# A conditional FFN on one core: first loads in another order, the last sequence's expert product inside its own wo, ranks turned two token tiles at a time

## The reference, cut to what matters

```python
# x: 8 sequences x 256 tokens x 256; F = 1024; rank 16; 8 experts; one expert id per sequence
h  = x @ wi.T
h += 2 * (x @ common_wi_a.T) @ common_wi_b.T
h += 2 * (x @ experts_wi_a[e].T) @ experts_wi_b[e].T      # e = expert of the sequence
h  = relu(h)
o  = h @ wo.T
o += 2 * (h @ common_wo_a.T) @ common_wo_b.T
o += 2 * (h @ experts_wo_a[e].T) @ experts_wo_b[e].T
return x + o
```

## Time and profile before

| | us |
|---|---|
| median of 3 runs (lowest, highest) | 123.06 (122.58, 123.3) |
| the profiled execution, its own time | 122.64 |
| its span, first to last instruction | 120.9 |
| PE busy | 113.3 |
| DVE, ACT, POOL busy | 53.5, 45.4, 41.2 |

### The profile page before, as it was taken

How to read it: one execution, slowest core, us unless ns; L and a number is a source line. 1 busy time by engine, 2 the same in 40 slices (tenths; PEclk the granted TensorE clock), 3 DMA queues, 4 the chain that set the end, 5 groups by cost and what they waited for, 6 DMA issues and landing times.

```text
span 120.9 us, 1964 instructions
## 1 busy us (share of the span) xinstructions
PE 113.3 (94%) x724; PEld 103.4 (86%) x724; DVE 53.5 (44%) x97; ACT 45.4 (38%) x93; POOL 41.2 (34%) x62
## 2 busy tenths in 40 slices
PE   6899949899999999999999999999999999999961
PEld 6688839678889999988889999988889999999950
DVE  4684899799954241134444331234444011111111
ACT  4552929944873411223663511313333111111120
POOL 2037761999999220215573005324000020200000
PEclk9999999999999999999999999999999999999999
DMA  2999899997480017106000025107000011111002
GB/s 85 384 242 350 285 384 346 386 304 249 98 319 0 5 46 217 35 11 217 0 5 0 0 57 163 43 5 216 1 0 0 0 46 46 43 43 42 22 22 87
DMA packets 8635, 14.52 MB, mean 120 GB/s; under 512 B 1026, under 2 KB 5122, under 8 KB 8626
## 3 DMA queue, kind: packets, MB, share of 16 engines
q1 hardware_dynamic: 7906, 13.09, 33.8%
q10 hardware_dynamic: 720, 1.31, 2.9%
HBM read 12.30 MB, written 2.10 MB: 119 GB/s over the span
## 4 chain that ended last, share of the span: by engine, by line
PE 76%; DVE 7%; ACT 6%; DMA 4%; SPq 4%; issue 1%; DVEq 0%
PE bank_o L654 40%; PE bank_h L567 23%; PE bank_h L601 5%; DMA b_raw<-in_rec_b 4%; DVE b_stack L458 3%; ACT hid L365 3%; ACT b_stack L353 2%; PE bank_o L673 2%; PE bank_low L618 2%; PE bank_o L567 1%; DVE low_stack L442 1%; PE bank_low L567 1%; DVE w_raw L480 1%; SPq L199 1%; PE bank_o L664 1%
## 5 line engine op out<-in xcount | busy, mean ns | idle before, releaser
L654 PE MATMUL bank_o<-wcat,hid 128*128 128x272 f32 x384 | 51.4, 290 | 0.0
L654 PEld LDWEIGHTS bank_o<-wcat,hid 128*128 128x128 f32 x384 | 49.7, 189 | 0.0
L567 PE MATMUL bank_h<-xT,wiT 128*128 128x512 f32 x156 | 39.7, 395 | 0.5 <-DVE wiT L512 0.5
L567 PEld LDWEIGHTS bank_h<-xT,wiT 128*128 128x128 f32 x156 | 28.1, 190 | 5.6 <-ACT xT L343 0.7
L442 DVE SCALAR_TENSOR_TENSOR hid<-bank_h,hid 128x512 fp32r<-128x512 f32 x26 | 17.3, 688 | 13.9 <-ACT hid L365 13.9
L502 DVE TENSOR_TENSOR o_sb<-bank_o,x_nat 128x256 f32<-128x256 f32 x16 | 6.8, 425 | 34.2 <-PE bank_o L673 34.2
L365 ACT ACTIVATE hid<-bank_h 128x512 fp32r<-128x512 f32 x26 | 14.8, 598 | 18.5 <-PE bank_h L601 18.2
L260 POOL TENSOR_TENSOR b_stack<-b_raw,b_stack 32x1024 fp32r<-32x1024 f32 x6 | 14.3, 2391 | 7.0 <-ACT b_stack L353 7.0
L278 POOL CAST wcat<-a_raw 128x128 fp32r<-128x128 f32 x8 | 2.3, 289 | 29.2 <-PE bank_o L654 29.1
L377 ACT ACTIVATE rank_sb<-bank_o 128x64 fp32r<-128x64 f32 x16 | 3.6, 225 | 22.3 <-PE bank_o L654 22.3
L601 PEld LDWEIGHTS bank_h<-low_stack,b_stack 128*128 128x128 f32 x52 | 8.7, 189 | 3.9 <-DVE low_stack L442 2.1
(11 more groups left out here) (50 smaller groups left out, 87.3 us busy)
## 6 DMA issues: line engine op xcount, KB each, us to landing
b_raw<-in_rec_b SPq DMA_DIRECT2D x8, 512.0 KB, 5.1
x_nat<-in_x_n SPq DMA_DIRECT2D x4, 512.0 KB, 5.3
out<-o_sb SPq DMA_DIRECT2D x16, 128.0 KB, 1.7
x_raw<-in_x_t SPq DMA_DIRECT2D x6, 256.0 KB, 3.2
w_raw<-in_wo_t SPq DMA_DIRECT2D x4, 256.0 KB, 6.1
w_raw<-in_wi_t ACTq DMA_DIRECT2D x3, 256.0 KB, 4.4
a_raw<-in_rec_a SPq DMA_DIRECT2D x8, 96.0 KB, 3.2
bo_raw<-in_rec_bo SPq DMA_DIRECT2D x8, 96.0 KB, 4.2
```

The costliest lines, as they stand in the source:

```text
L567: nc.tensor.matmul(up_bank(q, m)[:, :], wiT_at(sw, k, m), xT[q % 2][sx][:, k, :], start=start, stop=False)
L654: last = nc.tensor.matmul(bank_o[g % NO][:, 0:WIN], hid[q % 2][sh][:, m, tok], wcat[sw][:, m, win], start=(m == 0 and i == 0), stop=(m == ...
```

## The change

- **Loads.** SP issues the first half of wi before the expert ids. The three loads of `common` move from before `load_b(0)` to behind `load_a(1)`. On POOL `split_common` moves behind `split_a(1)`, and on DVE `common_b` moves from before the low parts of `b_stack` to behind the low parts of step 1's x.
- **Banks.** There are three `bank_h` and four `bank_o`; token tile t always uses `bank_o[t]`, and the up stages of steps 2 and 3 use `bank_o0` and `bank_o1` for tiles 3 and 4. `up_main(1, 1)` comes before `wo_product(0)`, and `wo_product(2)` and `(3)` behind `up_main(1, 2)`.
- **Turning by pairs.** `turn` runs once for two token tiles (ranks of both in one `rank_sb`), in the middle of the tile behind the pair, or for tiles 2 and 3 behind `ranks_in` or in the next step's first tile. Both `fin` of the pair follow. To pick a tile's ranks, `bo` is laid out as 512 columns with zeros (records of 96x512 in place of 96x256).
- **The last sequence.** `rec_ao` of the last sequence's expert is loaded into `common_raw`. In down 2 and down 3 eight matmuls `own_wo_product` make experts_wo_a x experts_wo_b, DVE adds it to what `w_raw` holds (wo with the common product), ACT and DVE split it into the no longer needed `wiT`. The last two token tiles then multiply with that wo: 256 columns, no ranks, no turn, no fin.
- `add` writes into `x_nat` in place, `o_sb` is gone, and `load_x_nat(q)` waits for the stores of step q - 2.

```diff
+            def load_last_ao():
+                sp.wait_ge(common_a_lo, 1)
+                sp.dma_start(common_raw[:, 0:F], rec_ao[bass.ds(expert[B - 1], 1), :, :].rearrange("o p c -> (o p) c")
+                             ).then_inc(last_ao_in, 16)
...
-            sp.dma_start(idt[:, :], ids.rearrange("(o n) -> o n", o=1)).then_inc(ids_in, 16)
             for k in range(KD):
                 sp.dma_start(w_raw[:, 0, k * 2 * P:(k + 1) * 2 * P], wi_t[0][:, k * 2 * P:(k + 1) * 2 * P]).then_inc(wi0_in[k], 16)
+                if k == 0:
+                    sp.dma_start(idt[:, :], ids.rearrange("(o n) -> o n", o=1)).then_inc(ids_in, 16)
...
+            def own_wo_product(i):
+                if i == 0:
+                    pe.wait_ge(last_ao_lo, 1)
+                    pe.wait_ge(bo_ready, B)
+                    pe.wait_ge(hid_lo, STEPS * MF)
+                for jj in range(2):
+                    m = 2 * i + jj
+                    last = nc.tensor.matmul(own_bank(i)[:, jj * D:(jj + 1) * D], common_st[:, m * P:(m + 1) * P],
+                                            bo_stack[(STEPS - 1) % 2][:, PAIR - 1, 0:D], start=True, stop=True)
                 last.then_inc(prod_done, 1)
...
             def down(q, before):
                 down_main(q, 0, FIRST_HALF)
                 if before is not None:
-                    turn(before, TT - 1)
+                    turn(before, 3)
+                    own_wo_product(3)
                 down_main(q, 0, SECOND_HALF)
                 if before is not None:
-                    fin(before, TT - 1)
-                for t in range(1, TT):
-                    down_main(q, t, FIRST_HALF)
-                    turn(q, t - 1)
-                    down_main(q, t, SECOND_HALF)
-                    fin(q, t - 1)
+                    fin(before, 2)
+                    fin(before, 3)
+                if q == 2:
+                    own_wo_product(0)
+                    own_wo_product(1)
+                down_main(q, 1)
+                down_main(q, 2, FIRST_HALF)
+                turn(q, 1)
+                if q == 2:
+                    own_wo_product(2)
+                down_main(q, 2, SECOND_HALF)
+                fin(q, 0)
+                fin(q, 1)
+                down_main(q, 3)
                 if q + 2 < STEPS:
                     ranks_in(q + 2, 0)
                     ranks_in(q + 2, 1)
-                    turn(q, TT - 1)
+                    turn(q, 3)
                     up_main(q + 2, 0)
-                elif q == STEPS - 1:
-                    turn(q, TT - 1)
-                    fin(q, TT - 1)
```

More of the change, by code:

```diff
@@ L15, with conditional_ffn @@
 STAGES = [("up", 0), ("up", 1), ("down", 0), ("up", 2), ("down", 1), ("up", 3), ("down", 2), ("down", 3)]
-def conditional_ffn(nc, x_t, x_n, ids, wi_t, wo_t, rec_a, rec_b, rec_bo, common, out):
+def conditional_ffn(nc, x_t, x_n, ids, wi_t, wo_t, rec_a, rec_b, rec_bo, rec_ao, common, out):
     P = 128
@@ L74, in up_bank_free @@
         def up_bank_free(q, m):
-            if q == 0:
+            if q == 0 or (q > 1 and m in (3, 4)):
                 return 0
@@ L196, in _ @@
                 load_a(0, n)
-            sp.wait_ge(common_zero, 1)
-            for i in range(3):
-                sp.dma_start(common_raw[i * BLK:i * BLK + R, :], common).then_inc(common_in, 16)
             load_b(0)
@@ L204, in _ @@
                 load_a(1, b)
+            sp.wait_ge(common_zero, 1)
+            for i in range(3):
+                sp.dma_start(common_raw[i * BLK:i * BLK + R, :], common).then_inc(common_in, 16)
             load_b(1)
@@ L518, in first_up @@
                     split_wi_lo(i)
-                common_b()
                 split_b_lo(0, 0)
@@ L524, in first_up @@
                     split_x_lo(1, k)
+                common_b()
                 for m in range(MF):
@@ L641, in down_main @@
                 if 0 in tiles:
-                    if t % SEQ_TILES == 0:
+                    if t % SEQ_TILES == 0 and not own_wo(g):
                         pe.wait_ge(ao_ready[b], q + 1)
-                    if g == 0:
-                        pe.wait_ge(hid_lo, MF + 4)
-                    if g >= NO:
+                    if q < STEPS - 1 and t < 2:
+                        pe.wait_ge(hid_lo, (q + 1) * MF + [3, 4][t] + (q > 0))
+                    elif g >= NO:
                         pe.wait_ge(added, g - NO + 1)
@@ L652, in down_main @@
                             pe.wait_ge(wo_lo, m // 2 + 1)
+                    if own_wo(g):
+                        if t % SEQ_TILES == 0 and m % 2 == 0:
+                            pe.wait_ge(wo_lo, PIECES + m // 2 + 1)
+                        for i, (sh, sw) in enumerate(((HI, HI), (HI, LO), (LO, HI))):
+                            last = nc.tensor.matmul(bank_o[t][:, 0:D], hid[q % 2][sh][:, m, tok], own_cols(sw, m // 2)[:, m % 2, :],
+                                                    start=(m == 0 and i == 0), stop=(m == MF - 1 and i == 2))
+                        continue
                     for i, (sh, sw) in enumerate(((HI, HI), (HI, LO), (LO, HI))):
-                        last = nc.tensor.matmul(bank_o[g % NO][:, 0:WIN], hid[q % 2][sh][:, m, tok], wcat[sw][:, m, win],
+                        last = nc.tensor.matmul(bank_o[t][:, 0:WIN], hid[q % 2][sh][:, m, tok], wcat[sw][:, m, win],
                                                 start=(m == 0 and i == 0), stop=(m == MF - 1 and i == 2))
@@ L711, in up @@
                     if m == 1:
+                        fin(before, TT - 2)
                         fin(before, TT - 1)
```

150 lines of the change are left out of this document (97 added, 53 removed).

## The result

The changed kernel is slower. Its median is 123.85 us (7 runs, 123.58 to 124.61) against 123.12 us for the kernel before on the same chip (7 runs), a ratio of 1.0087 with the interval [1.0047, 1.0127]. The forecast was 121.0 us, with 122.3 as the upper end of its range. Medians are over all runs, while the ratios leave out runs of a slower state (over 1.5% above the fastest of their kernel), so the two can differ. The execution that was profiled took 124.61 us and was the slowest of the seven; its span is 122.7 us, 1.8 us more than before.

What follows compares the result with a forecast made beforehand. PE, 94% busy at the full clock, was taken to set the time wherever it does not wait. Start -1.6, body -0.1, new wait +1.7 and tail -1.8 sum to -1.8: 122.85 - 1.8 = 121.0 us, range 119.4 to 122.3.

Steps and rivals of the forecast that it cites:

- The start: Up to up_lora(1, 0): earlier loads and the products 2 and 3 moved behind up matmuls give 1.6 us less.
- the third rival: At the start, common lands late and holds POOL up longer; slower than before, say 123.9 us; chance 0.04.
- One sign of being wrong: In the start: the forecast is wrong if hid_lo holds PE before 24 us.
- PE's body: PE's main work: eight turns fewer and narrower matmuls against eight own products, sum -0.1 us.
- The new wait: At ranks_in of step 3, PE waits 1.7 us for a_stack, whose reload stands behind step 1's first store.
- The tail: After the last main matmul: no turn, rank copies or fins of the last tile, 1.8 us less.
- The fourth: Rival: a wait in the own wo chain of down 2 or 3, about 1 us, 122.0; chance 0.09.
- The first, no new wait: Rival: a_stack of step 3 is in time after all, sum -3.5, about 119.3 us; chance 0.12.
- The second: Rival: the start gives only 0.4 to 0.9, common late or common_b caught by POOL, 121.8 to 122.4; chance 0.2.

Runs made afterwards that it cites:

- changed_again: The changed kernel without an edit, run again beside others of its group: 124.22 us, ratio 1.0076 to the kernel before.
- ids_first: The changed kernel with only the expert ids issued before the two halves of wi again: 123.42 us, ratio 0.9977.
- reload_ranks: reload_early plus, on DVE in the down stages, the ranks of tile 1 ahead of the second low part of x: 120.91 us, ratio 0.9801.
- ids_reload_ranks: reload_ranks with the expert ids issued first again: 119.68 us, ratio 0.9714.
- before_new_start: The kernel before with only the new order of loads, split_common and common_b: 123.28 us, ratio 1.0026.
- fill_no_own: fill without the last sequence's own wo; its last two token tiles go through ranks, turn and fin: 119.38 us, ratio 0.9717.
- fill_common_b: fill with DVE's common_b moved into the loop of the first hidden tiles, three tiles later: 120.66 us.
- fill: ids_reload_ranks with up_main(1, 2) ahead of up_lora(1, 0), up_lora(1, 1) right behind it, products 2 and 3 one tile later: 118.32 us, ratio 0.9593.
- ranks_first: The changed kernel with only DVE's ranks of tile 1 moved ahead of the second low part of x: 122.76 us, ratio 0.9984.
- reload_early: The changed kernel with step 3's a_raw reload issued ahead of the first store of step 1: 122.06 us, ratio 0.9952.
- start_as_before: ids_first with common also loaded, split and copied where the kernel before does it: 124.01 us, ratio 1.0055.

## Why the prediction was wrong, step by step

**The start** (forecast 1.6 us less, measured 0.7 more in the first trace and 0.2 less in the second) is the step that failed. It had `up_lora(1, 0)` at 24.5; it came at 26.74 and 25.87. Three things were wrong in it.

The first is its first sentence. I priced "the ids come about 0.4 us later (one DMA issue)". The issue did come 0.45 us later, but 32 bytes behind a load of 128 KB then took 2.37 us (the chain's row at 1.20), and 2.75 in changed_again. SP's reads of the ids, first before, then in the changed kernel:

```profile
L195 SPq TENSOR_LOAD <-idt x2: 274/373/472, 2.1 to 3.4; - x2
```

```profile
L213 SPq TENSOR_LOAD <-idt x2: 279/376/472, 3.6 to 4.9; - x2
```

So everything picked by the ids came 1.5 us late, which ate the whole 1.54 us that the moved `common` loads gave: `b_raw` issued at 6.17, not at 5.0. The issue of the last `common` began at 13.25; the 12.45 of the forecast is the end of that issue, so its start is 12.0, and it came 1.2 us late. Two pairs of kernels differ in the place of the ids alone (the changed kernel and ids_first, reload_ranks and ids_reload_ranks). By the ratios the ids cost 1.35 and 1.1 us there, at the gates of the traces 0.6 and 0.7. This is the largest part of the miss.

The second is an entry of POOL's list that no term has. The sum goes from the landing of `common` straight to POOL's 1.08 us, but `split_a(1)` stands in front, and waits for `a_raw` of step 1. In the changed kernel's trace:

```profile
17.52 0.32 POOL L273 TENSOR_TENSOR a_stack<-a_raw,a_stack 128x64 fp32r<-128x64 f32 x1
...
18.15 1.09 POOL L304 CAST common_st<-common_raw 96x1024 fp32r<-96x1024 f32 x1 [0.32 <-DMA common_raw<-in_common]
```

`split_a(1)` ends at 17.84, 1.9 us past the 15.9 at which the forecast has POOL begin with `common`, and POOL then waits only 0.3 us more. In changed_again, ids_first and before_new_start it does not wait for `common` at all. What this entry costs depends on when `a_raw` lands: in five traces with the ids first, POOL begins with `common` at 16.77 (ids_first), 16.59 (ids_reload_ranks), 16.20 (fill_no_own), 15.43 (fill_common_b) and 15.23 (fill), on both sides of the forecast 15.9. No run moves `split_a(1)` alone, so this part is read from traces and not from a comparison.

The third is the landing. The rows count it from the start of an issue, and the forecast added it to the end: from the start, "I take 15.9" leaves 3.9 us for the last `common`. It took 4.8 in the first trace, as long as the longest of the kernel before. It landed at 18.03, past the 17.7 that the third rival gave as the point where nothing is left, and that rival had a chance of 0.04. But its mechanism is the smallest part: POOL was not free before 17.84, so the landing cost 0.3 us in this trace and nothing in the second.

What came before the gate went as forecast. DVE's two low parts took 1.22 us each (forecast 1.35). In changed_again `up_lora(0, 0)` starts at 15.54 without a wait (forecast 15.4); in the first trace it starts at 17.81 because of slow matmuls (last section). One sign of being wrong that I had named did show: in changed_again `hid_lo` holds PE for 0.55 us at `ranks_in(1)`, at 19.54, because `common_b` ended at 18.67 and not before 17.5. The wait at the gate behind it hides that.

**The turns** are the step that was not there. Of the own wo I wrote that "I followed down 2 and down 3"; down 0 and down 1 I did not follow. There DVE has both low parts of step q + 2's x between the ranks of tile 0 and those of tile 1, and the second waits for ACT's `xT` copy, which stands behind ACT's own ranks of tile 1. While each tile had a turn of its own, a late `rank_sb` had half a tile to hide in; with pairs, the turn wants tile 1's ranks half a tile behind it. The timeline of the changed kernel shows the order:

```profile
44.47 0.77 DVE L487 TENSOR_TENSOR xT<-x_raw,xT 128x512 fp32r<-128x512 f32 x1 [2.04 <-ACT xT L360]
45.16 0.16 DVE L482 SCALAR_TENSOR_TENSOR rank_sb<-bank_o,rank_sb 128x16 fp32r<-128x16 f32 x1
```

The two downs take 0.48 and 0.34 us more than in fill, 0.8 together (0.9 in changed_again); ranks_first took them away and gained 0.87 in the trace.

**PE's body** was right: forecast -0.1. In fill, where PE does not wait from down 0 on, down 0 is 0.33 shorter than before, down 1 0.34, down 2 and 3 0.22 longer, up 2 and up 3 0.12 longer each for their second fin: -0.2 us.

**The new wait** was right in kind, place and cause, and within reach in size: forecast 1.7 (1.5 to 1.9), measured 2.11, and 1.56 in the second trace. The links are all there, from the add that lets the store go to the reload behind it and `a_stack` at last:

```profile
74.48 0.75 DVE L557 TENSOR_TENSOR x_nat<-bank_o,x_nat 128x256 f32<-128x256 f32 x2 [2.07 <-PE bank_o L768]
74.94 0.33 SPq L204 DMA_DIRECT2D out<-x_nat  x1
...
75.52 0.89 SPq L180 DMA_DIRECT2D a_raw<-in_rec_a  x2
...
78.85 0.34 POOL L270 CAST a_stack<-a_raw 128x192 fp32r<-128x192 f32 x1 [0.56 <-DMA a_raw<-in_rec_a]
```

The second record's load landed late here, with 0.56 us of POOL waiting between the two; in changed_again POOL went from one to the next at once. Taking the wait away gave 1.8 us (reload_early).

**The tail** was right: forecast 1.8 less, measured 4.49 - 2.65 = 1.84. The own wo as a whole is worth 1.1 us by the medians of fill_no_own and 0.9 in its trace, since its products cost PE on the way.

**The other rivals.** The fourth, a wait in the own wo's chain, did not come up: no row of waits names `wiT` in down 2 or 3. The first, no new wait, fell with the trace. The second was not the case in the changed kernel: DVE's operation took 1.14 us there, as in the earlier trace rows, beside POOL's short operation of 1.09 and not the long one. It did come in one execution of fill, whose lists have the same order there.

The terms as measured: start +0.7, body -0.2, turns +0.8, the reload's wait +2.1, `ranks_in` behind it +0.2 (1.19 against 0.96), tail -1.8. That is +1.8, and it is the difference of the two spans. In the second trace: start -0.2, body -0.2, turns +0.9, wait +1.6, `ranks_in` +0.2, tail -1.8, together +0.5. Between them lie the two sets of runs, with +1.1 and +0.9 us by their ratios. Against the forecast of -1.8 the start is the largest miss in both traces (2.3 and 1.4 us), the turns the second.

## What to carry to other kernels

Ask of each load what waits for its value, not how large it is: a few bytes that choose the addresses of later loads belong first on their queue, and their price is a landing behind whatever is ahead, not an issue. When a landing is followed into an engine, count every entry that stands ahead in that engine's list, with its own waits: here it was POOL's `split_a(1)` and not the landing that set the gate. When two steps are merged into one, the merged step wants the later of its inputs at the earlier time, so follow it in every stage in which it runs, with each other engine's list beside it, and not only in the stages where something new stands. A reload that waits in a list behind a store is tied to the stage that feeds the store; loads whose buffers come free earlier can stand ahead of it.

## What the runs showed of the hardware that was not expected

**The granted clock behind a pause.** Behind four pauses of PE the clock went to 0.50 (1.2 GHz) for some microseconds afterwards: 1.92 and 2.15 us (ids_first), 1.79 (ids_reload_ranks), 1.78 (fill_common_b). Behind others it stayed: 1.30 and 2.11 (the changed kernel), 1.92 (reload_ranks), 1.92 and 1.56 (changed_again), 1.38 and 1.60 (ranks_first), 1.62 (start_as_before). So the length of the pause alone does not tell. Where it fell, a wait cost 1.5 to 1.6 us more than its own length: from the gate to down 0 PE took 12.48 us in ids_first and 12.44 in ids_reload_ranks, against 10.91 in changed_again. None of this was in the forecast, which counted a wait at its length.

**Slow matmuls at a full granted clock.** In the changed kernel's own trace the first matmuls of 512 columns were slow, while the clock row reads nine tenths or more. The rows of the line, 4 to 10 us, first of the changed kernel, then of the same kernel in changed_again (durations min/median/max ns):

```profile
L640 PE MATMUL bank_h<-xT,wiT x13: 580/628/796, 4.5 to 9.8; 128*128 128x512 f32 x13
```

```profile
L640 PE MATMUL bank_h<-xT,wiT x18: 387/391/504, 4.9 to 8.9; 128*128 128x512 f32 x18
```

The kernel is the same, so it belongs to the execution. Weaker forms of it stand in the traces of start_as_before, reload_early and ranks_first (means of 479, 500 and 507 ns in that stretch, the clock at 1.00). It made `up_lora(0, 0)` 2.3 us later, but it did not set the gate: in reload_early `up_lora(0, 0)` was late as well, at 17.21, and `up_lora(1, 0)` came at 25.99, where changed_again has 15.54 and 25.87. What it is I can't say.

**DVE caught by POOL.** An operation of DVE on SBUF that starts while one of POOL on SBUF runs can be held until that one ends, and part of its own work then still follows. The 32x256 one ended 0.28 us behind POOL's in fill (19.37 against 19.09) and in the changed kernel (19.52 against 19.24); the 32x1024 one of before ended 1.08 us behind it (15.07 against 13.99, and the earlier trace rows). One with a single input was caught too (`TENSOR_SCALAR`, 1.41 us in place of 0.29, fill_common_b). When the loads land decides what meets what: with the same lists the 32x256 operation took 0.50 us in ids_reload_ranks, 1.14 in fill_no_own and 2.57 in fill.

**The last store** took 2.2 to 2.8 us to the end of the span in most traces and 3.4 and 3.7 in two, as much as any one edit here was worth.
